# Gathering the neighbour features of 24 row tiles while the last block is still computed, and redoing up to ten listed rows of each partition

## The chip, the cores and the metric

The kernel runs on one core of a Trainium2 chip. The metric is the device time of one execution in microseconds (us). The kernel before was timed three times: 1668.05 us median, 1666.44 to 1670.25. One more execution was recorded by the hardware profiler; it took 1673.38 us, of which the recorded span is 1671.6 us.

## The reference, cut to what matters

Two layers over 4096 rows of 512 numbers. Layer 0 is an attention whose scores get the matrix `adj` added twice. Layer 1 is a graph attention in which every pair without an edge of weight 1 is pushed down by -1e10 times its distance from 1, so that for each row one neighbour wins alone: the column at which the row of `adj` is largest.

```python
def reference(x, adj, ...):
    # layer 0
    a = q @ k.T * scale + adj + adj
    x = layernorm(x + softmax(a) @ v)
    # layer 1, per head h
    feats = x @ W[h]
    dense = leaky_relu(e_self[:, None] + e_neigh[None, :]) + (-1e10) * (1 - adj)
    x = layernorm(x + relu(concat_h(softmax(dense) @ feats) + b))
```

## The kernel before, in words

The 4096 rows are 32 tiles of 128 rows (tile t holds rows 128t to 128t+127, one per partition) and eight blocks of four tiles. Layer 0 runs block by block; each block takes 32 chunks, each the 128 keys of one tile against the 512 queries of the block. A loop over steps s (two chunks each) issues scores, the subtraction of a maximum, exponentials, a split of each number into a high and a low half-precision part, and the products with the values. `NCP` is 128, the number of steps in which scores are made; the value products lag by `LAG` = 18 steps. The last 12 chunks (`TAIL`) are multiplied after the loop, one 128-query quarter at a time: first all 12 chunks for O0, then for O1, O2, O3.

When a block is finished, its four tiles go through eviction and statistics on VectorE (DVE), a four-instruction scaling on GpSimd (POOL, `scale_of`), the normalisation on ScalarE (ACT, `unit_rows`), the split, eight transposes on TensorE (PE), the product with the layer 1 weights (`feats`), and an eviction with the bias (`evict_feats`). The result, the features of the tile, is stored to `feats_scratch`; the layer 0 rows are stored to `x1_scratch` (the profile writes `x_scratch`). The four tiles of the last block are called J0 to J3 (tiles 28 to 31).

Beside this, DVE scans `adj` row by row and leaves in `pick[:, t]` the column of the largest entry of each row of tile t. After layer 0 the end phase gathers, by an indirect DMA per tile issued from POOL, the feature rows that `pick` names (line 741), adds them to the layer 0 rows (DVE, line 1601), computes squares (ACT, line 1167), the square root (line 1170), five short corrections (DVE, lines 1575 to 1587), and normalises the even tiles on ACT (line 1160) and the odd ones on DVE (line 1591). SyncE stores the result (line 584), four tiles at a time, the last four in two groups of two. POOL waits, before its first gather, until all 32 tiles of features are in memory (`f_out`).

DVE also computes a number that shows whether every row has one neighbour that wins alone (`prove_single`, lines 1427 to 1438). If the sum of it is not 4096, a general path over all pairs runs instead; it does not run on these inputs.

The order on each engine is the order in which the code is written; an engine waits in place for the semaphores of its next instruction, and what stands behind it waits too. Line 719 is POOL's running sum of the exponentials, line 731 POOL's DMA that adds the bias of v onto the rows of x, line 526 SyncE's load of those rows, line 1404 DVE's split of the last 20 chunks, line 1388 the eviction of O, line 1411 that of the features, line 888 the transposes, line 1107 `unit_rows`.

## Time and profile before

| What | Value |
|---|---|
| Median of three runs | 1668.05 us (1666.44 to 1670.25) |
| Profiled execution, its own time | 1673.38 us |
| Its span | 1671.6 us |
| PE, DVE, POOL, ACT busy | 93%, 73%, 52%, 32% of the span |
| Last matmul | about 1602 us |
| First gather of the end phase | 1605.11 us |

The span is the stretch between the first and the last recorded instruction. The busy shares are averages over stages with different limits: up to 1602 us PE is nearly always busy, and from there to the end it does nothing.

### The profile page before, as it was taken

The page shows a single profiled execution, that of the slowest core. Times are in us where ns is not written, and L with a number is a line of the kernel's source. Part 1 is how long each engine was busy: PE and PEld are TensorE (multiplying, and loading weights), DVE is VectorE, ACT ScalarE, POOL GpSimd, SP SyncE. Part 2 cuts the span into 40 slices and gives each one's busy share as a digit, 9 for nine tenths or more (in the row PEclk, how much of TensorE's full clock was granted, in tenths as well). Part 3 has the DMA queues.
Part 4 walks back from the last instruction along what each step waited for, and adds up shares of the span by engine and source line. Part 5 has one row for each costly group of instructions (what it writes and reads, how often), then busy time and mean ns, then how long its engine had stood idle before and what let it go on. Part 6 is the DMA issues. An engine that isn't in the chain of part 4 may idle for free.

```text
span 1671.6 us, 27914 instructions
## 1 busy us (share of the span) xinstructions
PE 1558.7 (93%) x10052; PEld 968.3 (58%) x10052; DVE 1219.5 (73%) x2438; ACT 539.9 (32%) x822; POOL 865.6 (52%) x809
## 2 busy tenths in 40 slices
PE   7999998999999999999999999999999999989830
PEld 3444686666666666666666666666666666644310
DVE  5898687688867876687768876788578867846445
ACT  4556301222232223222322223223322232236336
POOL 2987402556454645554545554564455545667343
PEclk9999999999999999999999999999999999999965
DMA  7467886779757886798669866897589757757357
GB/s 264 167 249 279 294 297 208 226 246 287 256 183 252 294 280 187 232 304 257 217 206 312 280 215 203 283 304 235 180 269 326 233 184 253 241 189 233 88 152 283
DMA packets 192396, 403.24 MB, mean 241 GB/s; under 512 B 20736, under 2 KB 26880, under 8 KB 191104
## 3 DMA queue, kind: packets, MB, share of 16 engines
q1 hardware_dynamic: 182912, 376.25, 67.3%
q0 software_dynamic: 9344, 25.17, 5.9%
q8 instruction: 81, 1.33, 0.3%
q14 instruction: 59, 0.48, 0.1%
HBM read 343.67 MB, written 57.67 MB: 240 GB/s over the span
## 4 chain that ended last, share of the span: by engine, by line
PE 81%; DVE 5%; DMA 5%; POOL 3%; issue 2%; ACT 2%; SPq 1%; another core or an unknown queue 0%; DVEq 0%; POOLq 0%; ACTq 0%
PE O L845 33%; PE S L804 30%; PE O L759 6%; PE X L759 5%; DMA yb<-y_scratch 3%; PE S L759 2%; PE O L804 2%; PE BC L759 1%; POOL work L719 1%; POOL ring L741 1%; PE X L888 1%; DVE work L1362 1%; DVE xr L1388 1%; DVE ring L1404 1%; POOL ring L709 1%
## 5 line engine op out<-in xcount | busy, mean ns | idle before, releaser
L845 PE MATMUL O<-vring,ring 128*128 128x512 f16 x2928 | 707.3, 379 | 4.7 <-POOL ring L709 3.6
L804 PE MATMUL S<-yb,big 128*128 128x256 f16 x4974 | 621.2, 273 | 15.9 <-DVE ring L1336 7.2
L709 POOL TENSOR_TENSOR ring<-work,ring 128x512 f16<-128x512 f32 x236 | 282.3, 1196 | 601.9 <-ACT ring L1020 601.9
L804 PEld LDWEIGHTS S<-yb,big 128*128 128x128 f16 x4974 | 482.9, 98 | 168.6 <-DVE ring L1336 10.9
L845 PEld LDWEIGHTS O<-vring,ring 128*128 128x128 f16 x2928 | 286.3, 98 | 261.5 <-issue 7.6
L1141 ACT ACTIVATE work<-ring 128x512 f32<-128x512 f32 x256 | 160.8, 628 | 750.7 <-DVE ring L1327 717.4
L1336 DVE TENSOR_TENSOR ring<-S,ring 128x256 f32<-128x256 f32 x476 | 199.6, 419 | 219.3 <-PE S L804 216.2
L719 POOL TENSOR_TENSOR work<-work 128x512 f32<-128x512 f32 x248 | 342.9, 1383 | 7.0 <-ACT work L1141 5.9
L1362 DVE TENSOR_TENSOR work<-work,ring 128x512 f32<-128x512 f32 x248 | 209.1, 843 | 0.6
L1341 DVE TENSOR_TENSOR ring<-S,ring 128x256 f32<-128x256 f32 x357 | 150.6, 422 | 63.9 <-PE S L804 47.6
L1327 DVE TENSOR_TENSOR ring<-BC,ring 128x512 f32<-128x512 f32 x256 | 173.6, 679 | 1.8 <-PE BC L873 1.8
L1300 DVE MAX8 cand<-big 128x8 f32<-128x512 f32 x256 | 171.2, 683 | 3.3 <-DMA big<-in_adj 2.0
L1020 ACT ACTIVATE ring<-work 128x512 f16<-128x512 f32 x259 | 164.8, 637 | 10.8 <-POOL work L672 2.6
L1020 ACT ACTIVATE work<-X 128x1024 f16<-128x1024 f16 x28 | 28.7, 1024 | 180.1 <-PE X L888 180.1
L759 PE MATMUL O<-big,ring 128*128 128x512 f16 x384 | 84.2, 379 | 0.0
L759 PE MATMUL X<-yb,work 128*128 128x512 f16 x336 | 77.1, 379 | 0.0
L759 PEld LDWEIGHTS O<-big,ring 128*128 128x128 f16 x384 | 37.6, 98 | 45.3
L759 PEld LDWEIGHTS X<-yb,work 128*128 128x128 f16 x336 | 32.5, 98 | 34.9 <-ACT work L1020 1.2
L689 POOL DMA_INDIRECT work<-in_adj,wonrow x32 | 32.8, 1024 | 32.2 <-DVE wonrow L1310 31.6
L759 PE MATMUL S<-ring,big 128*128 128x512 f16 x192 | 42.8, 379 | 1.8 <-DVE big L1197 1.8
L804 PE MATMUL O<-yb,big 128*128 128x256 f16 x354 | 44.2, 273 | 0.0
L741 POOL DMA_INDIRECT ring<-feats_scratch,pick x32 | 32.2, 1005 | 20.6 <-DMA feats_scratch<-xr 11.2
(145 smaller groups left out, 1094.4 us busy)
## 6 DMA issues: line engine op xcount, KB each, us to landing
ring<-in_adjT SPq DMA_DIRECT2D x256, 256.0 KB, 4.6
big<-in_adj SPq DMA_DIRECT2D x256, 256.0 KB
big<-x_scratch SPq DMA_DIRECT2D x126, 512.0 KB, 4.4
vring<-v_scratch SPq DMA_DIRECT2D x244, 256.0 KB
yb<-y_scratch SPq DMA_DIRECT2D x56, 256.0 KB, 6.3
y_scratch<-yb SPq DMA_DIRECT2D x7, 1792.0 KB, 10.6
ring<-in_xT SPq DMA_DIRECT2D x8, 1024.0 KB, 6.7
v_scratch<-vring SPq DMA_DIRECT2D x32, 256.0 KB, 2.6
```

Of the source, the lines that this page charges most:

```text
L709: pool.tensor_tensor(ring16[:, e % SLOTS, 1, :], pf[:, e % NPF, :], ring16[:, e % SLOTS, 0, :], ALU.subtract).then_inc(lo_done, 1)
L719: pool.tensor_tensor(sacc, sacc, pf[:, e % NPF, :], ALU.add).then_inc(sum_done, 1)
L759: mm = pe.matmul(psum, sta(a, k), mov(b, k), start=(k + a + b == 0), stop=(k == n - 1 and a == 1))
L804: mm = pe.matmul(bank, keys_of(p, keys, a, c), yb[:, b % 2, queries, m, c, :], start=(start and c + a + m == 0), stop=(c == 1 and a == 1), ...
L845: mm = pe.matmul(O[j][:, :], ring16[:, e % SLOTS, a, j * P:(j + 1) * P], values_of(e)[:, m, :], start=(k + a + m == 0), stop=(k == NT - 1 ...
L1020: return nc.scalar.activation(dst, src, ACT.Copy, scale=scale)
L1141: nc.scalar.activation(pf[:, e % NPF, :], ring[:, e % SLOTS, :], ACT.Exp, scale=-2.0).then_inc(exp_done, 1)
L1300: dve.max(cand[:, q, :], piece[:, p % NSC, :]).then_inc(cand_set, 1)
L1327: dve.tensor_tensor(slot, BC[:, :], slot, ALU.subtract).then_inc(sub_done, 1)
L1336: dve.tensor_tensor(dst, banks(p)[0], dst, ALU.add).then_inc(chain_read, 1)
L1341: dve.tensor_tensor(dst, banks(p)[1], dst, ALU.add).then_inc(side_read, 1)
L1362: dve.tensor_tensor(mx, mx, slot, ALU.max).then_inc(max_done, 1)
```

## The change

Features of tiles 0 to 23 (`TE` = 24) are now gathered before the last block's features exist. A row whose neighbour lies in the last block (row 3584 or above) can't be served by that, so DVE lists, for each partition, up to ten (`LK`) such rows among the 24 tiles (`late_rows`). The early gather reads some other row in their place, and the early result for them is stored like the others. The listed rows are then done a second time: their layer 0 rows are gathered again (`gather_x1`), their features are gathered when all are there, they go through the same arithmetic as columns of a tile, and an indirect DMA scatters them into the output over the early result (line 822). Empty places of the list read a fixed row and have a target row out of bounds, which the scatter leaves out. If a partition has more than ten such rows, the proof's number is lowered, and the general path runs.

The end phase has now 42 columns: 24 early tiles (groups 0 to 5), 10 listed columns (groups 6 to 8, of 4, 4 and 2), and the 8 tiles 24 to 31 (groups 9 and 10). The result is written over the layer 0 rows rather than over the gathered ones. Square roots and corrections are done for units of groups: (0,1,2), (3,4,5), (6,7,8), (9), (10). Seven semaphores less and some more: the bias load of q now shares the semaphore of the load of Wv, the load of W1 that of the small loads.

On the inputs of the reference (seed 0), 363 of the 3072 early rows have their neighbour in the last block, at most 6 in one partition; 917 of the 1280 places of the list stay empty.

The DVE order in the loop, where the last block is under way: statistics of a tile, then the eviction of features of another. Before:

```order
L1197 SCALAR_TENSOR_TENSOR work<-xr,work 128x512
L1327 TENSOR_TENSOR ring<-BC,ring 128x512
L1394 BN_STATS stats<-xr 128x6
L1396 BN_AGGR mv<-stats 128x2
L1411 SCALAR_TENSOR_TENSOR xr<-X,b1b 128x512
L1327 TENSOR_TENSOR ring<-BC,ring 128x512
```

The same place now (lines are those of the changed kernel; 1499 to 1516 are the old 1394 to 1411). Ten of the 18 added instructions are shown:

```order
L1499 BN_STATS stats<-xr 128x6
L1501 BN_AGGR mv<-stats 128x2
L1561 CAST yb<-pick 128x24
L1562 TENSOR_SCALAR yb<-yb 128x24
L1563 TENSOR_SCALAR early_pick<-yb 128x24
L1564 CAST yb<-tile_i 128x24
L1565 TENSOR_TENSOR yb<-yb 128x24
L1566 TENSOR_TENSOR yb<-yb 128x24
L1567 MAX yb<-yb 128x8
L1568 MATCH_REPLACE yb<-yb 128x24
L1569 MAX yb<-yb 128x8
L1571 TENSOR_SCALAR late_tile<-yb 128x10
```

The list stands between the statistics and the eviction of features, and each of its instructions waits for the one before.

POOL after the loop's last sums, before: four times the scaling of a tile, then 32 gathers in a row.

```order
L719 TENSOR_TENSOR work<-work 128x512 x6
L696 TENSOR_TENSOR ve<-mv,eps 128x1
L698 TENSOR_TENSOR rstd<-ve,mhalf 128x1
L699 TENSOR_TENSOR nmean<-mv,mone 128x1
L701 TENSOR_TENSOR nmean<-nmean,rstd 128x1
```

POOL now, from the last scaling (that of J3) on:

```order
L734 TENSOR_TENSOR ve<-mv,eps 128x1 [waits mv_set]
L736 TENSOR_TENSOR rstd<-ve,mhalf 128x1 [waits scale_set]
L737 TENSOR_TENSOR nmean<-mv,mone 128x1
L739 TENSOR_TENSOR nmean<-nmean,rstd 128x1 [waits scale_set]
L791 DMA ring<-feats_scratch,early_pick 128x512 [waits e_sum]
L791 DMA ring<-feats_scratch,early_pick 128x512 x3
L746 DMA work<-x_scratch,late_src 128x512 x3
L746 DMA vring<-x_scratch,late_src 128x512 x3
L814 DMA ring<-feats_scratch,late_pick 128x512 [waits pv_done,f_out]
L814 DMA ring<-feats_scratch,late_pick 128x512 x9
L814 DMA ring<-feats_scratch,pick 128x512 x8
L822 DMA out<-yb,late_row 3072x512 [waits e_out_odd,e_out,early_out]
```

Sixteen early gathers now stand between the sums and the last scaling, eight more behind it, then six gathers of layer 0 rows; only then come the 18 gathers that need the last features, and behind them ten scatters.

DVE between the evictions of J0 and J1, now (line 1709 is an addition, 1302 the split, 1493 an eviction of O):

```order
L1302 SCALAR_TENSOR_TENSOR work<-big,work 128x512
L1709 SCALAR_TENSOR_TENSOR big,yb<-ring,big 128x512 x4
L1712 TENSOR_SCALAR yb<-yb 128x4
L1493 SCALAR_TENSOR_TENSOR xr<-O,rinv,xr 128x512
L1499 BN_STATS stats<-xr 128x6
L1501 BN_AGGR mv<-stats 128x2
```

Before, the eviction stood right behind the split; four additions and a short instruction are now between them, and the same between J1 and J2 and between J2 and J3.

The diff, cut to its core:

```diff
+    TE = 24
+    LK = 10
@@ groups
+        GROUPS = [range(e * 4, e * 4 + 4) for e in range(TE // 4)] + [range(TE, TE + 4), range(TE + 4, TE + 8),
+                                                                     range(TE + 8, TE + LK)]
+        GROUPS += [range(TE + LK, TE + LK + 4), range(TE + LK + 4, TE + LK + 8)]
+        UNITS = ((0, 1, 2), (3, 4, 5), (6, 7, 8), (9,), (10,))
@@ SyncE
+            for e, columns in enumerate(GROUPS):
+                if e < GE or e >= GS:
+                    first, n = row_tile(columns[0]), len(columns)
+                    sp.wait_ge(e_out, (columns[-1] + 1) // 2)
+                    sp.wait_ge(e_out_odd, (columns[-1] + 1) // 2)
+                    sp.dma_start(out[first * P:(first + n) * P, :].rearrange("(j p) n -> p j n", p=P),
+                                 x1r[:, first:first + n, :]).then_inc(early_out if e < GE else out_done, 16)
@@ POOL, in the loop
+                if NCP + 9 <= s < NCP + 13:
+                    gather_x1(s - NCP - 9)
@@ POOL, behind the loop
-            for j in range(JB):
-                scale_of(NT - JB + j)
+            def gather_early(e):
+                if e == 0:
+                    pool.wait_ge(f_out, (NT - JB) * 16)
...
+                if e >= 3:
+                    pool.wait_ge(e_sum, GROUPS[e - 3][-1] + 1)
+                for c in GROUPS[e]:
+                    pool.indirect_dma_start(out=gathered(c), out_offset=None, in_=f_d[0:N - QB, :],
+                                            in_offset=bass.IndirectOffsetOnAxis(ap=early_pick[:, c:c + 1], axis=0)
+                                            ).then_inc(got_in[e], 16)
+            gather_early(0)
+            scale_of(J0)
+            gather_early(1)
+            scale_of(J1)
+            gather_early(2)
+            scale_of(J2)
+            gather_early(3)
+            scale_of(J3)
+            gather_early(4)
+            gather_early(5)
+            for k in range(4, LK):
+                gather_x1(k)
             pool.wait_ge(f_out, NT * 16)
...
+            pool.wait_ge(early_out, 16 * GE)
+            for e in range(GE, GS):
+                pool.wait_ge(e_out, (GROUPS[e][-1] + 1) // 2)
+                pool.wait_ge(e_out_odd, (GROUPS[e][-1] + 1) // 2)
+                for c in GROUPS[e]:
+                    pool.indirect_dma_start(out=out[0:TE * P, :],
+                                            out_offset=bass.IndirectOffsetOnAxis(ap=late_row[:, c - TE:c - TE + 1], axis=0),
+                                            in_=home(c), in_offset=None, bounds_check=TE * P - 1, oob_is_err=False
+                                            ).then_inc(late_moved, 16)
@@ ACT
             copy_transposed(first)
+            act.wait_ge(rinv_set, NB)
+            squares(0)
             unit_rows(first + 1, x1r[:, first + 1, :])
+            squares(1)
             copy_transposed(first + 1)
             unit_rows(first + 2, x1r[:, first + 2, :])
+            squares(2)
             unit_rows(first + 3, x1r[:, first + 3, :])
             copy_transposed(first + 2)
             copy_transposed(first + 3)
+            deviations(0)
+            squares(3)
+            squares(4)
+            squares(5)
+            deviations(1)
+            normalise(0)
+            squares(6)
+            normalise(1)
+            squares(7)
+            squares(8)
+            deviations(2)
+            squares(9)
+            deviations(3)
+            normalise(2)
+            squares(10)
+            deviations(4)
+            normalise(3)
+            normalise(4)
@@ DVE, in the loop
+                if s == NCP + 4:
+                    late_rows()
@@ DVE, behind the loop
             unit_rows_lo(J0, x1r[:, J0, :])
+            additions(0)
             evict(NB - 1, 1)
...
+            additions(1)
             evict(NB - 1, 2)
...
+            additions(2)
             evict(NB - 1, 3)
             statistics(J3)
             evict_feats(J0)
             unit_rows_lo(J3, x1r[:, J3, :])
             evict_feats(J1)
+            additions(3)
             evict_feats(J2)
             evict_feats(J3)
+            additions(4)
+            additions(5)
+            normalise_odd(0)
+            additions(6)
+            normalise_odd(1)
+            additions(7)
+            additions(8)
+            additions(9)
+            normalise_odd(2)
+            additions(10)
+            normalise_odd(3)
```

## Rows read from the trace of the kernel before

**Rows 1.** The page: its first line, and part 4, shares of the chain.

```profile
span 1671.6 us, 27914 instructions
PE 81%; DVE 5%; DMA 5%; POOL 3%; issue 2%; ACT 2%; SPq 1%; another core or an unknown queue 0%; DVEq 0%; POOLq 0%; ACTq 0%
```

**Rows 2.** Windows: length, busy PE, PEld, DVE, ACT, POOL (count), clock, DMA share, GB/s.

```profile
1610.00:1615.00 5.00, 0.00 (x0) 0.00 (x0) 2.06 (x7) 0.00 (x0) 3.78 (x5) 0.50 0.74 211
1640.00:1645.00 5.00, 0.00 (x0) 0.00 (x0) 0.96 (x6) 3.22 (x9) 3.78 (x5) 0.50 1.02 389
1655.00:1660.00 5.00, 0.00 (x0) 0.00 (x0) 4.72 (x17) 4.97 (x14) 0.00 (x0) 0.50 0.56 210
```

**Rows 3.** Timeline, 1596 to 1666: start, length, engine, line, what, idle before.

```profile
1596.28 0.62 PE L888 MATMUL S<-ident,work 128*128 128x128 f16 x8
...
1602.12 0.69 DVE L1411 SCALAR_TENSOR_TENSOR xr<-O,b1b 128x512 f32<-128x512 f32 x1 [1.90 <-PE O L759]
...
1605.11 1.11 POOL L741 DMA_INDIRECT ring<-feats_scratch,pick  x1 [11.18 <-DMA feats_scratch<-xr]
...
1612.94 0.69 DVE L1601 SCALAR_TENSOR_TENSOR ring<-ring,big 128x512 f32<-128x512 f32 x1 [10.13 <-DMA ring<-feats_scratch,pick]
...
1613.56 0.69 DVE L1601 SCALAR_TENSOR_TENSOR ring<-ring,big 128x512 f32<-128x512 f32 x1
...
1664.98 0.81 ACT L1160 ACTIVATE ring<-ring,yb 128x512 f32<-128x512 f32 x1 [0.31 <-DVE yb L1587]
```

**Rows 4.** The gathers, line 741, and the output stores, line 584: ns min/median/max.

```profile
L741 POOL DMA_INDIRECT ring<-feats_scratch,pick x32: 945/949/1402, 1605.1 to 1645.6; - x32
DMA to landing us min/median/max: 3.5/3.7/3.8
L584 SPq DMA_DIRECT2D out<-ring x9: 372/372/389, 1625.3 to 1665.8; - x9
```

**Rows 5.** Timeline, 1499 to 1504, where the list is put.

```profile
1499.81 3.83 PE L845 MATMUL O<-vring,ring 128*128 128x512 f16 x17
1500.87 0.18 DVE L1396 BATCH_NORM_AGGREGATE mv<-stats 128x2 f32<-128x6 f32 x1
1500.97 0.69 DVE L1411 SCALAR_TENSOR_TENSOR xr<-X,b1b 128x512 f32<-128x512 f32 x1
1503.48 0.61 PE L888 MATMUL X<-ident,work 128*128 128x128 f16 x8
```

**Rows 6.** Timeline, dependent short DVE instructions: at 1251 and 1524.

```profile
1251.05 0.22 DVE L1304 MAX8 top<-cand 128x8 f32<-128x64 f32 x1
1251.37 0.09 DVE L1306 MATCH_VALUE_LOAD wonq<-top,cand 128x8 f32 x1
1524.43 1.07 DVE L1430 TENSOR_SCALAR yb<-top 128x64 f32<-128x64 f32 x1
1526.53 0.19 DVE L1436 TENSOR_TENSOR yb<-yb 128x32 f32<-128x32 f32 x1
1526.76 0.19 DVE L1437 TENSOR_TENSOR yb<-yb 128x32 f32<-128x32 f32 x1
```

**Rows 7.** Timeline, 1547 to 1560, before the last quarter products.

```profile
1547.52 1.47 POOL L719 TENSOR_TENSOR work<-work 128x512 f32<-128x512 f32 x1 [0.21 <-ACT work L1141]
1548.11 1.75 SPq L526 DMA_DIRECT2D xr<-in_x  x4
1554.23 1.38 POOL L731 DMA_DIRECT2D xr<-in_bv  x1 [5.24 <-DMA xr<-in_x]
```

**Rows 8.** Timeline, 1565 to 1591: J0, and the eviction of J3.

```profile
1565.22 1.05 PE L856 MATMUL X<-vup,work 128*128 128x1 f32 x8 [0.22 <-POOL work L719]
...
1568.37 0.19 POOL L696 TENSOR_TENSOR ve<-mv,eps 128x1 f32<-128x1 f32 x1 [3.21 <-DVE mv L1396]
...
1574.12 0.62 PE L888 MATMUL S<-ident,work 128*128 128x128 f16 x8
...
1590.84 0.75 DVE L1388 SCALAR_TENSOR_TENSOR xr<-O,rinv,xr 128x512 f32<-128x512 f32 x1 [2.83 <-PE O L845]
```

More of the change, by code:

```diff
@@ new lines, in adj_resnorm_kernel, with row_tile @@
+        e_s = end[:, 384:384 + 64]
+        e_r = end[:, 448:448 + 64]
+        e_t = end[:, 512:512 + 64]
+        e_nm = end[:, 576:576 + 64]
+        e_tot = end[:, 640:640 + 64]
+        okw = end[:, 1024:1024 + 8 * NT]
+        late = end[:, 1280:1536]
+        def row_tile(c):
+            return c if c < TE else c - LK
+        x1s = [end[:, 1536 + D * k:1536 + D * (k + 1)] for k in range(4)]
+        x1s += [mx, diag.rearrange("p j n -> p (j n)"), won]
+        x1s += [vring[:, k].rearrange("p a n -> p (a n)").bitcast(F32) for k in range(NV)]
@@ L579, in _ @@
             store_feats(J3)
[L580 to L586 removed]
+            for e, columns in enumerate(GROUPS):
[5 more added lines that the diff above has]
+                                 x1r[:, first:first + n, :]).then_inc(early_out if e < GE else out_done, 16)
+            sp.wait_ge(early_out, 16 * GE)
+            sp.wait_ge(out_done, 16 * (NE - GS))
+            sp.wait_ge(late_moved, 16 * 2 * LK)
             for j in range(JB):
```

236 lines of the change are left out of this document (141 added, 95 removed).

## The prediction

> **What bounds the kernel now.** I read the page first, then the windows of the end, then the timeline of the hand-over. The chain of waits is PE for 81% of the span [rows 1]: until the last matmul the kernel is bound by PE, and work added beside PE costs nothing unless PE waits for it. Behind it comes an end phase of another kind. The last feature eviction starts at 1602.12, the first gather at 1605.11, when the features are in memory, and the span ends at 1671.6: 66.5 us without a matmul [rows 1, 3]. In it POOL issues 32 gathers, the first at 1605.1, the last at 1645.6: 40.5 / 31 = 1.31 us from one to the next, though one is busy for 0.95 only [rows 4]. DVE makes its first addition at 1612.94, waiting for a gather [rows 3]. The DMA engines are not full at first (211 GB/s at 1610), are full at 1640 (share 1.02, 389 GB/s) and half full at 1655 [rows 2]. So the end is bound first by POOL's issue, then by DMA, then by ACT and DVE, with a last store at 1665.8 that ends 5.8 us later [rows 1, 4]. The change starts this phase 40 us earlier for three quarters of the tiles, and adds 20 indirect DMAs and 10 columns of arithmetic.
>
> All times below are on the clock of the profiled execution.
>
> **Part 1, the list on DVE: +3.7 us.** Eighteen dependent instructions are put between the statistics and the eviction of features, at 1501.05 [rows 5]. No row shows one of them in this place. Dependent short ones follow each other by 0.23 us (1526.53 to 1526.76), and by 0.32 where a pause instruction stands between, as it does in the list (1251.05 to 1251.37) [rows 6]. I take 0.30, nearer to the second: 5.4 us. Behind them the eviction of features waits, and for it the transposes of the next tile, on PE in order. The eviction ended at 1500.97 + 0.69 = 1501.66, while PE has matmuls until 1503.4 [rows 5]; the cover is 1.7 us. PE waits 5.4 - 1.7 = 3.7 us and has no slack to win it back before the load of x for the last block, which is released by PE's progress. Low end: 18 x 0.23 - 1.7 = 2.4. High end: 18 x 0.32 and one slow first instruction, as the 1.07 us one in the proof (0.9 over its likes) [rows 6]: 5.8 + 0.9 - 1.7 = 5.0. The two steps added to the proof (0.5 us) fall where DVE is not waited for by PE.
>
> **Part 2, four gathers of layer 0 rows inside the loop: 0.** They cost POOL 4 x 1.31 = 5.2 us between its last sums. POOL has 0.21 us idle before each sum there, and 5.24 us of idle time before line 731, where it waits for x [rows 7]. Eight sums' idle time takes 1.7, the other 3.5 lie in the 5.24. SyncE issues the load by PE's progress, so POOL's delay does not move it. That leaves 1.2 us of cover.
>
> **Part 3, early work beside the last block's tiles: 0, though the features come 3.5 us later.** POOL is free at 1565.2, and the first statistics reach it at 1568.37 [rows 8]. Four gathers end at 1570.5, so the scaling of J0 is 2.1 us late; its rows, split, are ready just when PE reaches their transposes at 1574.12. On DVE a group of additions is 4 x 0.62 (1612.94 to 1613.56) + 0.2 = 2.7 us [rows 3]. Walking DVE, ACT and POOL in their new order, the evictions of J1, J2 and J3 start at 1577.0, 1585.1 and 1594.0 (the last was 1590.84 [rows 8]). PE does not wait for J1 and J2; the transposes of J3 go from 1596.28 to 1599.4 [rows 3], and the last features reach memory at 1608.6 and not 1605.1. This is hidden by the next part, which is later.
>
> **Part 4, POOL's way to the gathers that matter: +10.3 us.** J3's scaling can end at 1597.1 (statistics 1595.8, scaling 1.3). Behind it stand eight early gathers and six of layer 0 rows: 14 x 1.31 = 18.3, so the 18 gathers that need the last features start at 1615.4, not at 1605.1. Here the queue has turned into the bound: 3.3 of the 10.3 would be the features' own lateness anyway.
>
> **Part 5, from there to the end: 47.1 us and not 66.5, -19.4 us.** 18 gathers take 23.6: until 1639.0. But POOL then waits for the early stores. The first three (ACT normalises after the squares of groups 3 to 5) can go at 1620.7, the next three at 1633.3. From 1620.7 DMA has 6 x 1.05 MB of stores and 14 gathers x 0.26 MB, 9.9 MB, at 389 GB/s [rows 2] 25.5 us; with a landing, 1646.7. The listed columns are normalised at about 1645.9, so the store is what releases. Ten scatters at the gather's 1.31 start until 1646.7 + 9 x 1.31 = 1658.5 and land 3.7 later [rows 4], 1662.2, the end at 1662.5. The last store (four tiles, ready at 1651.9) lands by 1659.2, taking the old 5.8 us plus 1.5 for twice the bytes: it isn't the last. The scatter is an operation that before does not show. From below it is 0.95 us, POOL's busy time for a gather; then that store ends the kernel, -3.3 us. From above twice a gather, 2.6 us: +11.6 us. I take the gather's.
>
> The Trainium skill (DMA: Bandwidth & Descriptors, Bandwidth) puts the HBM side at about 358 GB/s per core. The row of 389 GB/s is above it, so the trace does not agree here; by the page's figure part 5 would end 2.2 us later, by an estimate.
>
> The merged semaphores in the first 20 us I cost at nothing: the bias waits now for Wv, behind PE's first product.
>
> **Sum.** +3.7 + 10.3 - 19.4 = -5.4 us: 1673.38 - 5.4 = 1668.0 for an execution like the profiled one. That one is 5.3 us above the median of the timed runs, so I put the same difference on the median: 1668.05 - 5.4 = 1662.6 us.
>
> **Rivals.** (a) The scatter is dearer than a gather: it has a bound to check per row. From 1.31 + 5.4 / 9 = 1.9 us each the gain is gone; at 2.6 it is 1662.6 + 11.6 = 1674.2 us, slower. For it speaks that all ten stand alone at the very end, with nothing beside them. Against: seven in ten of their rows move nothing. Chance 0.18. (b) The stores don't get 389 GB/s. That rate stood in the fullest stretch only; 9.9 MB at 320 GB/s take 31 us and end 5.4 later: 1668, no change. Gathers in the same queues then land later too. Chance 0.17. (c) More is won: the list costs 2.4 and scatters 0.95 each: 1662.6 - 1.3 - 3.3 = 1658 us. For it speaks that empty rows of a scatter make no transfer. Chance 0.22. (d) The cover of part 2 fails, since the list delays DVE, ACT and POOL more than it does PE: POOL reaches the x load later than the load lands, up to 3.5 us, and each late us moves the whole end: 1666. Chance 0.05. (e) The change does not do what it says, and the general path runs: it needs more than ten listed rows in a partition, and the inputs have at most 6. Chance 0. The forecast keeps 0.38.
>
> **The numbers.** A measurement of this kernel can tell about 0.2%, 3.3 us. Faster by more: nearly all of the forecast (0.33), (c), and 0.03 of the others: 0.57. Within: 0.05 of the forecast, most of (b) and of (d): 0.22. Slower by more: (a), and the worst of (b) and (d): 0.21. The forecast's own range is 1659 to 1666; the range from (c) with something over to where (a) is at 2.5 us each is 1655 to 1673.
>
> **What would show it.** In the profile after: DVE's list of about 5.4 us before the eviction of features at 1501, and PE idle for 3.7 before the transposes behind it; POOL still idle before line 780 (old 731); the 18 late gathers starting at about 1619 (1615.4 + 3.7); early stores issued at about 1624 and 1637; the ten scatters last on POOL, 1.3 us apart, from about 1650; a span of 1666. I am wrong if the scatters are far from 1.3 us, if PE does not wait behind the list, or if ACT or DVE and not POOL's scatters end the kernel.

## The result and the profile after

The changed kernel takes 1687.41 us (median of four runs) against 1669.15 for the kernel before (four runs, 1666.44 to 1671.62). One of the four, at 2112.58 us and a lower clock, was disturbed and is left out of the ratio; the others lie between 1683.43 and 1687.67. The ratio is 1.0102, with a 95% interval of 1.0084 to 1.0119: the kernel is slower by 1%, 25 us above the forecast of 1662.6. The profiled execution took 1683.43 us and has a span of 1681.6, where the one before had 1673.38 and 1671.6 [rows 1].

Walk along the same marks as the forecast did. The first is the list. The timeline of the changed kernel (start, length, engine, line, operation):

```profile
1500.47 0.32 DVE L1561 CAST yb<-pick 128x24 f32<-128x24 uint32 x1
1500.72 1.27 POOL L766 TENSOR_TENSOR work<-work 128x512 f32<-128x512 f32 x1
1500.90 1.12 DVE L1562 TENSOR_SCALAR yb<-yb 128x24 f32<-128x24 f32 x1
1501.94 1.16 POOL L756 TENSOR_TENSOR ring<-work,ring 128x512 f16<-128x512 f32 x1
1502.13 1.01 DVE L1563 TENSOR_SCALAR early_pick<-yb 128x24 uint32<-128x24 f32 x1
1503.06 1.26 POOL L766 TENSOR_TENSOR work<-work 128x512 f32<-128x512 f32 x1
1503.24 1.12 DVE L1564 CAST yb<-tile_i 128x24 f32<-128x24 int32 x1
1504.46 0.18 DVE L1565 TENSOR_TENSOR yb<-yb 128x24 f32<-128x24 f32 x1
...
1506.24 0.17 DVE L1572 CAST yb<-late_tile 128x10 f32<-128x10 int32 x1
...
1508.52 0.69 DVE L1516 SCALAR_TENSOR_TENSOR xr<-X,b1b 128x512 f32<-128x512 f32 x1 [0.17 <-DVE late_src L1581]
1509.36 1.01 PE L970 MATMUL X<-ident,work 128*128 128x128 f16 x8 [5.85 <-DVE xr L1516]
```

Eighteen steps take 8.0 us (1500.47 to 1508.52), not 5.4. Fifteen of them follow each other by 0.28 us or a little more. Lines 1562, 1563 and 1564 take 1.0 to 1.1 us each, although they touch 24 elements, and each ends within 0.1 us of the end of POOL's long addition or subtraction beside it. PE waits 5.85 us for the eviction of features, where before it waited for nothing [rows 5], and behind that wait it runs at the lower of its two clocks, 1.2 GHz (granted clock 0.50 from 1509 to 1513, 1.00 from there): six matmuls in 2.77 us instead of 1.46. The second mark is the hand-over to the last quarter products, the answer to [rows 7] and to the first row of [rows 8]:

```profile
1542.64 1.15 DVE L1509 TENSOR_TENSOR ring<-work,ring 128x512 f16<-128x512 f32 x1
1543.41 1.32 POOL L746 DMA_INDIRECT yb<-x_scratch,late_src  x1 [0.17 <-POOL work L766]
1544.32 2.29 DVE L1509 TENSOR_TENSOR ring<-work,ring 128x512 f16<-128x512 f32 x1
...
1555.43 1.75 SPq L560 DMA_DIRECT2D xr<-in_x  x4
...
1562.87 1.42 POOL L780 DMA_DIRECT2D xr<-in_bv  x1 [2.03 <-DMA xr<-in_x]
1563.35 2.80 DVE L1509 TENSOR_TENSOR ring<-work,ring 128x512 f16<-128x512 f32 x1 [0.16 <-ACT ring L1102]
...
1574.08 1.05 PE L938 MATMUL X<-vup,work 128*128 128x1 f32 x8 [0.22 <-POOL work L766]
```

POOL still has 2.03 us of idle time before line 780, which adds bv, though no longer 5.24. DVE's line 1509 takes 2.29 us when a gather of POOL stands beside it, 1.15 beside POOL's sums, and 0.68 at 1561.92, where POOL does nothing. The row sums come at 1574.08 instead of 1565.22. The third mark is the end phase, the answer to [rows 2 to 4]:

```profile
1616.17 0.69 DVE L1516 SCALAR_TENSOR_TENSOR xr<-O,b1b 128x512 f32<-128x512 f32 x1 [1.90 <-PE O L841]
...
1624.56 0.94 POOL L814 DMA_INDIRECT ring<-feats_scratch,late_pick  x1 [0.30 <-issue]
...
1659.19 1.51 ACT L1245 ACTIVATE yb<-yb 128x512 f32<-128x512 f32 x2
...
1663.53 1.03 POOL L822 DMA_INDIRECT out<-yb,late_row  x1 [16.04 <-DVE big L1738]
...
1675.19 0.98 POOL L822 DMA_INDIRECT out<-vring,late_row  x1 [0.30 <-issue]
```

In windows (length, busy PE, PEld, DVE, ACT, POOL, clock, DMA share, GB/s):

```profile
1625.00:1630.00 5.00, 0.00 (x0) 0.00 (x0) 2.63 (x6) 4.90 (x11) 3.78 (x5) 0.50 0.90 201
1640.00:1645.00 5.00, 0.00 (x0) 0.00 (x0) 1.06 (x3) 4.83 (x8) 3.90 (x4) 0.50 1.04 222
1655.00:1660.00 5.00, 0.00 (x0) 0.00 (x0) 4.79 (x16) 4.28 (x11) 0.00 (x0) 0.50 1.00 391
```

The lines of the late gathers (L814) and of the scatters (L822); the MOVE is what POOL's queue runs ahead of each scatter:

```profile
L814 POOL DMA_INDIRECT ring<-feats_scratch,late_pick x10: 942/946/1316, 1624.6 to 1636.3; - x10
DMA to landing us min/median/max: 5.0/9.4/12.5
L822 POOLq MOVE  x10: 29/29/29, 1662.2 to 1667.8; - x10
L822 POOL DMA_INDIRECT out<-vring,late_row x3: 985/987/987, 1672.6 to 1675.2; - x3
DMA to landing us min/median/max: 2.1/3.6/6.7
```

Late gathers land 9.4 us after their issue (median), where before they took 3.7. The first scatter starts 39.0 us behind the first late gather; ten of them start 1.29 us apart, as forecast; the span ends 6.4 us after the last start.

The profile's name for what released the first scatter (DVE's line 1738) can't be right, for that instruction ends at 1663.46 and POOL's queue has been past its waits since 1662.2. By the kernel, POOL waits there for the six early stores and then for the listed columns of the first group only, two of which ACT normalises. ACT has done the second of them at 1660.70 (1659.19 + 1.51). The DMA engines move the last bytes of the stores between 1661.5 and 1662.0 (share 0.07, then 0.00). So the stores are what comes last here, by 1.5 us, as the forecast had it, and the first scatter starts 1.3 us behind the release.

One more thing is new: from 1625 to 1660 the DMA engines are busy all the time (share 0.90 to 1.04), but move 201 GB/s at 1625 and 222 at 1640, against 391 at 1655 with the same share.

**e8_after_again.** The changed kernel was run again beside the experiments.

> The changed kernel itself, beside the same runs of the kernel before: ratio 1.010 as on the other chip, if the loss does not hang on the chip. In its profile the waits at the list (PE 5.9 us), before the row sums, and at the first scatter (16 us) should come again.

Measured on another chip: 1689.34 us (4 runs), ratio 1.007 (1.0052 to 1.0089), so the loss is there again, somewhat smaller. The experiments ran on four chips, each beside runs of the kernel before, so ratios and not times are compared. So that profiles can be compared, I count from one mark ahead of the list, the start of the two matmuls S<-usum (1483.60 before, 1483.11 after). Each figure is the difference of two starts in the timeline, in us:

| kernel | mark to row sums | to last feature eviction | to first late gather | to first scatter | to last scatter | to the end |
|---|---|---|---|---|---|---|
| before | 81.6 | 36.9 | 3.0 (first gather) | | | 66.5 |
| after | 91.0 | 42.1 | 8.4 | 39.0 | 11.7 | 6.4 |
| after, second profile (e8) | 91.9 | 44.5 | 5.8 | 44.6 | 11.6 | 6.5 |
| e1 spread | 91.8 | 41.2 | 8.4 | 38.8 | 11.7 | 6.4 |
| e2 list split | 83.1 | 43.6 | 6.9 | 39.9 | 11.8 | 6.4 |
| e10 thin stores | 90.7 | 41.2 | 8.5 | 38.8 | 11.6 | 6.5 |
| e12 spread, thin stores | 92.2 | 43.6 | 6.9 | 40.2 | 11.6 | 6.5 |
| e15 list split, pause | 84.7 | 42.2 | 11.7 | 38.8 | 11.6 | 6.4 |
| e5 six places | 84.9 | 46.3 | 3.8 | 33.3 | 6.5 | 7.8 |
| e7 six, spread, order | 83.1 | 43.8 | 5.2 | 32.7 | 6.6 | 8.1 |
| e9 six, stores sooner | 82.8 | 43.6 | 5.0 | 29.9 | 7.0 | 9.0 |

### The profile page after: what moved, and what is told of

Read it like the earlier page. It is cut to its first block and busy times, and to the rows that moved or that the text cites. A ratio compares the mean times of both kernels' runs of the same rounds, so it can differ in the third digit from the quotient of the medians.

```text
span 1681.6 us, 28033 instructions
## 1 busy us (share of the span) xinstructions
PE 1563.7 (93%) x10052; PEld 970.2 (58%) x10052; DVE 1239.5 (74%) x2466; ACT 552.2 (33%) x843; POOL 895.8 (53%) x840
## 5 line engine op out<-in xcount | busy, mean ns | idle before, releaser
L841 PEld LDWEIGHTS O<-big,ring 128*128 128x128 f16 x384 | 37.6, 98 | 45.3
L927 PE MATMUL O<-ring 128*128 128x512 f16 x144 | 35.4, 399 | 7.0 <-DVE ring L1509 7.0
```

What stands on the lines that cost most here:

```text
L841: mm = pe.matmul(psum, sta(a, k), mov(b, k), start=(k + a + b == 0), stop=(k == n - 1 and a == 1))
L927: mm = pe.matmul(O[j][:, :], ring16[:, e % SLOTS, a, j * P:(j + 1) * P], values_of(e)[:, m, :], start=(k + a + m == 0), stop=(k == NT - 1 ...
```

## Experiments on the list and inside the loop

**e2_list_split.** The changed kernel with the list in two halves of nine steps, behind DVE's first subtraction of the next two steps instead of ahead of an eviction:

```diff
-                if s == NCP + 4:
-                    late_rows()
+                subtract(e)
+                if s in (NCP + 5, NCP + 6):
+                    late_rows(s - NCP - 5)
```

> The changed kernel, but the 18 instructions of the list stand in two halves of nine behind the first subtraction of steps NCP+5 and NCP+6, where DVE was idle for 5.4 us in the kernel before. Theory (the list costs what PE waits behind it): PE's wait of 5.9 us before the transposes at 1509 is gone, and with it the 1.3 us of half clock behind it; the last sums end 6.5 to 7.5 us earlier, and so does the kernel. Rival (the list is hidden anyway by the load of x, POOL's sums or the early gathers, and moving it only moves the wait): less than 2 us.

Measured: 1679.12 us (10 runs), ratio 1.0019 (1.0006 to 1.0032). From the mark to the run of 108 matmuls behind the list it is 40.9 us (1487.40 to 1528.33), as before (1483.60 to 1524.57, 41.0), against 48.8 in the changed kernel (1483.11 to 1531.89). So the list in one piece cost 7.8 us of the path, and in two pieces nothing. Its trace also settles why three steps are slow. The CAST of tile_i took 1.12 us at 1503.24 above; here it is line 1566:

```profile
1508.57 0.18 POOL L735 TENSOR_TENSOR ve<-mv,eps 128x1 f32<-128x1 f32 x1
1508.74 0.18 DVE L1566 CAST yb<-tile_i 128x24 f32<-128x24 int32 x1
...
1514.99 1.15 POOL L757 TENSOR_TENSOR ring<-work,ring 128x512 f16<-128x512 f32 x1
1515.16 1.01 DVE L1574 CAST yb<-late_tile 128x10 f32<-128x10 int32 x1
```

The same CAST takes 0.18 us beside a short instruction of POOL. The CAST of late_tile, 0.17 us at 1506.24 above, takes 1.01 now that it has fallen beside POOL's line 757. Not the operation, but POOL's 128x512 work at the same time makes a step 1.1 us long. The Trainium skill (SBUF — State Buffer, "Who interferes with whom") states that copies, casts and tensor_scalar of DVE in their two-port modes take a pair of ports that it shares with GpSimd, as an exclusive lock for a whole instruction, so that whoever comes second waits until the first is done; the rows agree, each of the three ending with POOL's instruction. Row sums still come 1.5 us later than before (83.1 against 81.6), which is the price of what else the change puts there: the four gathers inside the loop and two more steps in the proof.

**e3_x1_sooner.** The changed kernel with those gathers four steps sooner:

```diff
-                if NCP + 9 <= s < NCP + 13:
-                    gather_x1(s - NCP - 9)
+                if NCP + 5 <= s < NCP + 9:
+                    gather_x1(s - NCP - 5)
```

> The changed kernel, but the four gathers of layer 0 rows in the loop stand at steps NCP+5 to NCP+8, where POOL waits for ACT, and not at NCP+9 to NCP+12 between its last sums. Theory (each of the four holds DVE's split of a chunk, 2.2 us instead of 1.16, and the delay outlasts the load of x): the row sums come 1 to 2 us earlier, the kernel 1 to 2 us. Rival (their cover holds, as I costed it): no change within 0.5 us.

Measured: 1686.43 us (4 runs), ratio 1.0063 (1.0042 to 1.0083), not to be told from the changed kernel's 1.007 of e8. From the run of 108 matmuls to the row sums it is 42.7 us (1534.38 to 1577.08), no less than 42.2 after, and 40.7 before. Their place among POOL's last sums is not what costs the 1.5 us.

## Experiments on the end phase

**e4_before_one_row.** The kernel before, with eight of its 32 gathers (tiles 4 to 11) reading one and the same row in all partitions:

```diff
+                    rows = one_row[:, 0:1] if 4 <= t < 12 else pick[:, t:t + 1]
-                                            in_offset=bass.IndirectOffsetOnAxis(ap=pick[:, t:t + 1], axis=0)
+                                            in_offset=bass.IndirectOffsetOnAxis(ap=rows, axis=0)
```

> The kernel before, but the eight gathers of tiles 4 to 11 read row 4095 in all 128 partitions in place of their picks, so these tiles of the result are not the reference's. It measures the price of reading one row by itself: the gathers stand early in the end phase, when DMA is not full (211 GB/s before). Theory (one row is slow): they land in 6 us or more, DMA share is near 1 at 200 GB/s or less, and the end comes 5 us or more later. Rival: they land in 3.7 us as the others, no change.

Measured: one execution, 1678.43 us with a span of 1676.6. Its time shows nothing, for the kernel before had a median of 1676.85 (1670.95 to 1679.15) beside it. The first gather starts at 1603.24, so it is 73.4 us from there to the end, against 66.5 in the first profile of the kernel before and 70.2 in its second (e14 below). Nor is all of that the price of one row: in this profile DVE stands still from 1631.9 to 1646.7 but for a few short instructions, a thing that comes up again below and that the profiles of the kernel before have too, for 8.5 and 12 us. What comes ahead of it is the gathers' own: the third and the fourth group of additions start 21.5 and 26.2 us behind the first gather, against 18.2 and 23.9 in both profiles of the kernel before, 2.3 to 3.3 us later. The windows of this kernel:

```profile
1615.00:1620.00 5.00, 0.00 (x0) 0.00 (x0) 2.52 (x8) 3.33 (x8) 3.78 (x5) 0.50 0.94 155
1620.00:1625.00 5.00, 0.00 (x0) 0.00 (x0) 2.19 (x11) 4.64 (x11) 3.83 (x4) 0.50 0.89 202
```

The engines are 0.94 and 0.89 busy for 155 and 202 GB/s, where before had 0.69 and 0.72 for 201 and 197. A gather of one row by 128 partitions holds the engines longer for the same bytes.

**e1_spread.** The changed kernel, with empty places of the list pointing at rows that differ from partition to partition (three steps more):

```diff
+                then(dve.tensor_scalar(filler, top[:, 0:LK], 0.0, -1.0, ALU.is_equal, ALU.mult))
+                then(dve.scalar_tensor_tensor(out=none, in0=filler, scalar=rowf[:, :], in1=none, op0=ALU.mult, op1=ALU.add))
```

> The changed kernel, but what fills an empty place is another row for each partition: an empty place of the list reads feature row 4095 - 8p (about) and layer 0 row p instead of 4095 and 3071 for all, and an early row with a late neighbour reads the row 512 above it instead of 3583. Three more short instructions in the list (+0.8 us). Theory (many reads of one row are slow, whatever the engines' busy share says): from 1635 to 1645 DMA moves over 370 GB/s and not 222 to 301, the late gathers land within 6 us instead of up to 12.5, the wait before the first scatter falls from 16 us to 9 or less, and the time falls by 5 to 8 us against the changed kernel. Rival (the low rate comes from stores and gathers in one queue, or from the number of gathers): the rates stay, the time rises by 0.8 us.

Measured: 1688.68 us (4 runs), ratio 1.0081 (1.006 to 1.0101): no gain. Early rows with a late neighbour and the empty places of the layer 0 gathers are spread in the same way (not shown in the cut). The slow transfers are gone:

```profile
1635.00:1640.00 5.00, 0.00 (x0) 0.00 (x0) 3.17 (x7) 4.91 (x10) 3.78 (x5) 0.50 1.04 395
1640.00:1645.00 5.00, 0.00 (x0) 0.00 (x0) 2.12 (x7) 1.76 (x3) 3.78 (x5) 0.50 1.03 404
```

395 and 404 GB/s, against 301 and 222 after, and no transfers from 1655 on (share 0.05). So the stores no longer come last: POOL's queue is past its waits at 1660.4, right behind the end of ACT's second listed normalisation at 1660.29. Yet the first scatter stays 38.8 us behind the first late gather, for ACT itself waits 8.10 us at 1649.87 for DVE, which between 1642 and 1649.7 starts an instruction each 1.40 us and then none for 2.80 us.

**e10_thin_stores.** The changed kernel, with the six early stores writing 8 of 128 rows of each tile:

```diff
+                    m = 8 if e < GE else P
-                                 x1r[:, first:first + n, :])
+                                 x1r[0:m, first:first + n, :])
```

> The changed kernel, with the six early stores writing 8 of 128 rows of each tile, so 0.4 MB instead of 6.3 MB; the other rows of those tiles are left out. Theory 1 (the full DMA engines are why the late gathers land late, the stalls of DVE and ACT come and the first scatter waits): late gathers land in under 4 us as in the kernel before, no stall stands on DVE from 1634 to 1655, the first scatter starts as soon as ACT has normalised the list, some 31 us behind the first late gather as forecast, not 39 to 45, and the span is 8 to 10 us shorter than with whole stores. Theory 2 (the gathers of one row hold the engines by themselves): DMA share stays near 1 with under 250 GB/s from 1625 to 1645, and at most 3 us are won.

Measured: one execution, span 1681.7, first scatter 38.8 us behind the first late gather (the 37.5 in the expectation of e12 counts from the second gather, a slip of mine), so no gain from 5.9 MB less. Without the stores ACT's normalisation is what comes last: it ends at 1662.21, POOL's queue goes on at 1662.3. But ACT comes 37.4 us behind the first late gather here, against 36.1 in the changed kernel, and DVE starts one instruction each 1.40 us or none from 1636 to 1639.6 and again from 1644 to 1651.6, as in e1 and unlike in the first profile of the changed kernel. What thin stores bring without that, this run does not show.

**e11_no_scatters.** The changed kernel without its ten scatters. 

> The changed kernel with the ten scatters left out, so the listed rows keep what the early stores wrote. It gives what the scatters cost at the end, where they stand alone. Forecast's view: ten scatters of 1.29 us and their landing are all that stands behind the last store, which is issued at about 1669: the span becomes that issue and 6 us, 5 to 7 us less than with them. Other view: SP's last waits and the end of the program take the 6.4 us between the last scatter's start and the end, scatter or store alike, and less than 5 us are won.

Measured: span 1677.9, 196.1 us from the mark, against 198.5 and 204.8 in the two profiles of the changed kernel. The last store is issued at 1670.9 and the span ends 7.0 later. With scatters it was issued at 1669.6 and the span ended 12.0 later: they cost 5 us at the end, as the first of the two views had it. This profile has the standstill of e1 too (1634.1 to 1645.2), so the spans themselves can't be compared to a microsecond.

**e12_spread_thin.** Both edits together. 

> The changed kernel with ten places, with both suspects of the end phase gone: empty places read spread rows, and the early stores write 8 of 128 rows of each tile (the rest of those tiles is left out). Neither alone brought more than 2 us. Theory 1 (either of the two is enough to fill the DMA engines, so only both together free the end): no window from 1625 to 1650 shows a DMA share over 0.8, late gathers land in under 4 us, DVE has no stall, and the first scatter starts 31 us behind the first late gather, as forecast (39.0 in the changed kernel, 38.8 with spread reads, 37.5 with thin stores): some 7 us less than the changed kernel, ratio near 1.003. Theory 2 (DVE and ACT stand still in this stretch for a reason that isn't the transfers): stalls of 5 us or more stay in DVE's rows with the engines half empty, and the first scatter stays over 36 us behind.

Measured: 1687.11 us, ratio 1.0073 (1.005 to 1.0096), first scatter 40.2 us behind. The windows and the timeline of DVE:

```profile
1635.00:1640.00 5.00, 0.00 (x0) 0.00 (x0) 1.10 (x5) 0.00 (x0) 3.78 (x5) 0.50 0.71 233
1640.00:1645.00 5.00, 0.00 (x0) 0.00 (x0) 0.57 (x4) 3.25 (x8) 3.78 (x5) 0.50 0.73 206
```

```profile
1635.34 0.69 DVE L1716 SCALAR_TENSOR_TENSOR yb<-ring,yb 128x512 f32<-128x512 f32 x1
...
1639.93 0.17 DVE L1719 TENSOR_SCALAR yb<-yb 128x4 f32<-128x4 f32 x1 [3.90 <-remote]
...
1642.74 0.17 DVE L1727 SCALAR_TENSOR_TENSOR yb<-yb 128x12 f32<-128x12 f32 x1 [2.51 <-issue]
1644.13 0.17 DVE L1730 SCALAR_TENSOR_TENSOR yb<-yb 128x12 f32<-128x12 f32 x1 [1.22 <-DVE yb L1727]
1645.53 0.17 DVE L1733 SCALAR_TENSOR_TENSOR yb<-yb 128x12 f32<-128x12 f32 x1 [1.23 <-DVE yb L1730]
1646.93 0.17 DVE L1737 SCALAR_TENSOR_TENSOR yb<-yb 128x12 f32<-128x12 f32 x1 [1.23 <-DVE yb L1733]
1648.34 2.83 DVE L1745 TENSOR_SCALAR big<-big,yb 128x512 f32<-128x512 f32 x6 [1.24 <-issue]
```

The engines are used to 0.71 and 0.73 only, and DVE stands still all the same: for 3.90 us with nothing to wait for that the profile shows, and then one instruction each 1.40 us, chained 128x12 instructions that follow each other by 0.2 us elsewhere. ACT resumes at the same instant, 1648.34. POOL starts its last gather at 1647.21; after it all is quick again. The kernel before shows the like, unremarked by me at the forecast: from 1637.6 to 1646.1 its DVE runs six short instructions and nothing else, and this lies in its 66.5 us.

**e14_before_again** and **e13_before_pause.** The kernel before once more, and the kernel before with a break of 4 us on POOL behind its 16th gather:

```diff
+                if e == 4:
+                    pause()    # 3 x pool.tensor_tensor(sacc, sacc, sacc, ALU.subtract), each waited for
```

> The kernel before itself, for a second profile of it. Theory 1: DVE's standstill comes again at the same place, after 25 or so gathers. Theory 2 (chance of the execution): it is gone, longer, or elsewhere.

> The kernel before, with three dependent additions of 128x512 on POOL, some 4 us, between its 16th and 17th gather. In its profile DVE and ACT stand still from 1637.7 to 1646.1 with their semaphores reached, starting one instruction per 1.40 us, and the stretch begins some 25 gathers after POOL began to issue them without a break. Theory 1 (a long unbroken row of indirect DMAs brings the standstill, whether the engines are full or not): the break takes it away, DVE shows no idle time put to nothing, and the end comes no later than before, although 16 gathers start 4 us later: ratio 0.998 to 1.000. Theory 2 (it comes by chance of the execution, or by DVE's place in its program): it stays, and the 4 us are lost: ratio 1.0025.

Measured: e14 has the standstill at the same place, from 1639.0 to 1651, 26 gathers into the row; span 1676.6. In e13 it is gone, and from the first gather to the end it is 64.3 us, against 66.5 and 70.2 with the standstill. 1673.65 us (12 runs) with a ratio of 0.9991 (0.9975 to 1.0006) say the same without a profile: the 4 us of delay came back. The window of 1640 to 1645, first of e14, then of e13:

```profile
1640.00:1645.00 5.00, 0.00 (x0) 0.00 (x0) 0.00 (x0) 0.00 (x0) 3.78 (x4) 0.50 1.03 402
```

```profile
1640.00:1645.00 5.00, 0.00 (x0) 0.00 (x0) 4.44 (x16) 1.87 (x5) 3.88 (x4) 0.50 1.01 367
```

DVE and ACT run nothing for 5 us in the one, and 16 and 5 instructions in the other, both with full DMA engines (1.03 and 1.01).

**e15_split_pause.** The same break in the kernel of e2, ahead of its 18 late gathers. 

> The changed kernel with the list in two halves (ratio 1.0019 by itself), and the same 4 us break on POOL between its 14 gathers behind J3's scaling and the 18 late ones. By itself POOL issued 32 without a break, and DVE stood still from 1631.6 to 1642. Theory 1: the standstill goes, the first scatter starts 31 us behind the first late gather instead of 39.9, and with the 4 us lost the kernel is 4 to 5 us faster than without the break: ratio 0.999. Theory 2: it stays, and 4 us are lost: ratio 1.004.

Measured: 1680.69 us (12 runs), ratio 1.0033 (1.0019 to 1.0046). The standstill is gone, but the time isn't: DVE waits 9.4 and 1.8 us for late gathers, and the engines move 198 and 151 GB/s at a share of 1.00 and 0.99 from 1635 to 1645. Here the stores come last again: ACT's second listed normalisation ends at 1657.08, the DMA engines are done by 1659 (share 0.58, 0.07 and 0.00 in the microseconds from 1657), and POOL's queue goes on at 1659.0. The first scatter is 38.8 us behind, as in e1. The kernel that would settle it, with spread reads and the break, was not built.

## Fewer places: a version that is faster than both

**e5_six**, **e6_six_spread**, **e7_six_order**, **e9_store_sooner.** All have the list in two halves, and six places instead of ten (the inputs need six; a seventh sends a partition's rows to the general path):

```diff
-    LK = 10
+    LK = 6
-        UNITS = ((0, 1, 2), (3, 4, 5), (6, 7, 8), (9,), (10,))
+        UNITS = ((0, 1, 2), (3, 4, 5), (6, 7), (8,), (9,))
```

e6 adds the spread reads of e1; e7 lets ACT and DVE normalise the listed columns ahead of the next four tiles; e9 also normalises the first twelve tiles sooner:

```diff
             squares(3)
+            normalise(0)
             squares(4)
             squares(5)
             deviations(1)
-            normalise(0)
```

> The list has room for six rows of a partition instead of ten (the inputs need six at most), and is made in two halves as in the experiment before; 16 steps, for the second maximum and its replacement aren't needed. Four gathers of layer 0 rows, four gathers of features, four scatters and four columns of arithmetic are gone. Theory 1 (the end is bound by how many indirect DMAs POOL issues one after another): the late gathers start 4 x 1.26 = 5.0 us sooner and the scatters are 4 x 1.29 = 5.2 us shorter, together 10.2 us: 1669 us of span against 1679.1 with ten, ratio to before 0.996. Theory 2 (the first scatter is set by transfers and by ACT, the four layer 0 gathers are hidden): only the scatters' 5.2 us are won: span 1674, ratio 0.999. Theory 3 (the last store and not the scatters then ends the kernel): a gain between the two, and the last DMA to land is that store.

> The same with six places, and empty places of the list read rows spread over the tensor instead of one row. Theory 1 (reads of one row by 128 partitions are what holds the DMA engines at 200 GB/s): of six columns at least three are nearly empty, so those 2 x 3 gathers land sooner, the windows from the early stores on show 380 GB/s or more, and the end comes 2 to 4 us sooner than with six places alone: ratio 0.994. Theory 2 (ACT's and DVE's order sets the first scatter): DMA rates rise but the end stays within 1 us of the kernel with six places alone.

> The kernel before it, with ACT and DVE normalising the listed columns before they take the first four tiles of the last block, not behind them. Theory 2: the first scatter waits for ACT, so it starts about 3.4 us sooner (four squares of 0.85), and the end 2 to 3 us sooner, until the last store ends it. Theory 1: the first scatter waits for the early stores to land, and nothing changes; the last store comes later by the time that was moved, 1 to 2 us, which costs as much if it is the end.

> The kernel with six places, spread reads and the listed columns normalised first; ACT now normalises the first twelve tiles before the squares of group 4 and DVE its half behind the last feature eviction. In the kernel before it ACT idles 5.5 us at 1608.5 and the DMA engines are used to 0.32 from 1615 to 1620, while the first early store is issued at 1622.6 and all stand full from 1625 to 1645. Theory 1 (the first scatter waits for the early stores, 1648.6): the first three stores are issued about 8 us sooner, DMA is done about 6 us sooner, the first scatter starts at about 1642 and the last store, bound by ACT, ends the kernel: 3 to 5 us less, ratio to before 0.990 to 0.991. Theory 2 (stores and late gathers then collide sooner, and the gathers, on which DVE waits, land later by what the stores win): no change, ratio 0.993.

| kernel | median us, runs | ratio to before, interval |
|---|---|---|
| e5_six | 1667.27, 5 | 0.9938, 0.9923 to 0.9953 |
| e6_six_spread | 1666.17, 5 | 0.9932, 0.9917 to 0.9948 |
| e7_six_order | 1665.37, 5 | 0.9933, 0.9916 to 0.9950 |
| e9_store_sooner | 1665.37, 5 | 0.9932, 0.9918 to 0.9946 |

The kernel before had a median of 1677 us beside them. From the first late gather to the end e5 takes 47.6 us and e7 47.3, where after took 57.0. Six places bring 0.8% over ten (0.9938 against 1.0019), some 13.6 us, more than the 10.2 us of issue that were counted: in all four profiles POOL has 3.7 to 4.2 us of idle time ahead of its late gathers, since it waits for the last features, and DVE and ACT do not stand still behind it. (The two ratios come from two chips.) In all four the early stores release the first scatter, 3.0 to 8.9 us behind ACT's normalisation, which is why e7's new order of ACT brings nothing. Spread reads, the order of ACT and earlier stores each move a row of the profile as expected and the time by less than can be measured. In e9 the first store goes at 1613.9 instead of 1622.6 and the window of 1615 to 1620 fills:

```profile
1615.00:1620.00 5.00, 0.00 (x0) 0.00 (x0) 4.79 (x17) 4.75 (x13) 3.37 (x3) 0.50 0.32 79
```

```profile
1615.00:1620.00 5.00, 0.00 (x0) 0.00 (x0) 4.96 (x16) 1.62 (x4) 2.19 (x2) 0.50 1.00 370
```

From 79 (e7) to 370 GB/s (e9); but DVE then waits 7.5 us for the first late gathers instead of 3.4, behind those stores in the same engines, and the rival of that expectation is right.

## Why the forecast was wrong

**Bounds.** Right: up to the last matmul PE is the bound, and each microsecond put on it (list, clock, gathers) reached the end.

**Part 1, the list: +3.7 forecast, +7.8 measured** (48.8 against 41.0 from the mark). Mechanism right, size wrong twice. The range for the list ended at 5.8 us and allowed for one slow first instruction; 15 steps went at 0.28 and three at 1.1, beside POOL. The row of 1.07 us in [rows 6] was the hint: I read it as a first instruction that is slow, when a neighbour on POOL is what makes one slow. And after 5.85 us of waiting PE runs some 2 us behind at half its clock, which the sum left out.

**Part 2, gathers in the loop: 0 forecast, 1.5 measured.** The cover held: POOL still waits 2.03 us for x before line 780. (The forecast's own numbers leave 5.24 - 3.5 = 1.7 us of it, not 1.2.) So rival (d), by which POOL would come later than the load, did not happen in this profile. What the sum left out is the load itself. It is issued 23.5 us behind the start of the 108 matmuls in both kernels (1548.11 and 1555.43), but POOL goes on 7.44 us behind its issue instead of 6.12. That is 1.3 of the 1.5 us, and e2 has the same 7.45. It is not so everywhere: in e1 and e10 POOL goes on 6.25 and 5.66 us behind the issue, and the row sums come 18.7 and 18.2 us behind it all the same, against 17.1 before. So the 1.5 us are there in all of them, and which wait they lie in is not settled.

**Part 3, beside the last block: features 3.5 us later forecast, 5.2 measured** (42.1 against 36.9), 1.2 of it because 24 matmuls of the last features ran partly at the lower clock (6.53 us instead of 5.34, granted clock 0.80 from 1610 to 1615). It stood behind part 4 and was hidden, as said.

**Part 4, POOL's way: right.** From the row sums to the first late gather the forecast had 50.2 us (1615.4 less 1565.22), the profile has 50.5.

**Part 5 is the step that failed: 47.1 us from the first late gather to the end forecast, 57.0 measured.** Scatters at 1.31 each: right (1.29), so rival (a) did not happen. Their tail: 6.4 us behind the last start, not 4.0; the forecast let the landing of a gather stand for that of a scatter and for the end of the program. The rest, 7.7 us, lies ahead of the first scatter, and the term that failed is the transfers of the early stores. The forecast had them issued 5.3 and 17.9 us behind the first late gather, and the profile has 4.2 and 17.5. It gave 9.9 MB 25.5 us at 389 GB/s. The profile has 10.95 MB between 1628.8 and 1662.0, at a mean of 330 GB/s: 33.2 us, for the windows of 1635 and 1640 bring only 301 and 222. So the release comes 37.6 us behind the first late gather and not 31.3, and the scatter starts 1.3 us behind its release, which no term had. This is rival (b), with its place, its size (320 GB/s) and its sign that gathers land later (9.4 us); it had a chance of 0.17, and it did not know why the rate falls.

The 358 GB/s that the forecast takes from the Trainium skill (DMA: Bandwidth & Descriptors, Bandwidth) is there a core's share while both cores of its pair stream. This kernel runs on one core, so the row of 389 does not speak against the page.

The second term ahead of the first scatter failed as well, and was hidden by 1.5 us only. It had the listed columns normalised 30.5 us behind the first late gather; ACT has done those of the first group 36.1 us behind it, in e10 37.4, in e1 37.3. So there are two ways to the first scatter, the stores and the chain of late gather, addition, square and normalisation, and both are some 6 us too long. Two things stretch them: reads of one row by the empty places (after, e15), which slow the stores and the late gathers, and the standstill of DVE and ACT in a long row of gathers (e1, e10, e12), which slows the chain. The second profile of the changed kernel has both, and 44.6 us. Taking one away let the other set the end, which is how I read that e1, e10, e12 and e15 brought nothing. Each of the two is shown by itself: the standstill goes with a break on POOL (e13, e15), the low rate goes with spread rows (windows of e1). That the two together are the whole of the loss is argued and not shown, for no kernel with ten places has neither, and 31 us were never seen with ten.

**The account.** The profiled span was to become 1666.2 (1671.6 - 5.4) and became 1681.6, 15.4 us more: row sums 8.9 later instead of 3.7 (+5.2), part 4 +0.3, first scatter +7.7, scatters -0.1, tail +2.4, together 15.5. The timed median is off by 24.8 us (1687.41 - 1662.6), and the other 9.4 lie outside this profile. The forecast took 5.3 us off, since the profiled execution of the kernel before was slower than the median; that of the changed kernel is 4.0 us faster than its median (1683.43). It is also the only one of its two profiles without the standstill, so the others may well have had it; their times alone can't show that.

**What stays open.** What the standstill is. It came in both profiles of the kernel before, after 26 gathers without a break, and in that of e4 after 23; in seven of the eight profiles of kernels with ten places and no break, some 24 gathers into the row behind J3's scaling (e1, e2, e3, e8, e10, e11, e12); it did not come in the first profile of the changed kernel, whose row is as long, nor in any where POOL paused for some 4 us. A shorter one, of 2.9 to 5.1 us, stands ahead of one of the last two feature evictions in the profiles of e3, e5, e6, e7, e8, e10 and e11, also some 22 gathers behind POOL's first early one, though there with breaks of 2 to 3 us in between; it makes the second column of the table vary. A queue that fills would look so, but no row shows one. It is seen in recorded executions only; that it is no effect of the recording rests on the times of e13. Open too are what the 1.5 us of part 2 are made of, and what ten places cost with spread reads and a break.

## What to carry to other kernels

Short dependent instructions on DVE cost what POOL is doing beside them: price them at the row of the neighbour (1.1 us here), not at their own 0.2, and put them where DVE's successors are not waited for. An indirect DMA for places that are empty is not free: it costs its issue, its arithmetic and, when all partitions point at one row, engine time; the first thing to cut was the number of places, worth 0.8%. When two waits end within 1.5 us of each other, taking one away shows nothing of its price. And before a stage is timed by its parts, look at whether its rows hold idle time that nothing explains: a stage that has 8 us of it will not shrink as the sum says.

## What the runs showed of the chip that was not expected

- Gathers in which all partitions read one row of 2 KB: eight of them made the additions behind them start 2.3 to 3.3 us later (e4), with DMA share 0.94 at 155 GB/s; spread rows brought 395 and 404 GB/s (e1) where one row had 301 and 222.
- DVE and ACT standing still for some microseconds, then or in between one instruction each 1.40 us, 5 to 15 us in all, behind some 23 to 26 indirect DMAs that POOL issued without a break; gone with 4 us of other work on POOL between them (e13, e15), with the DMA engines as full as before.
- DVE's 128x512 TENSOR_TENSOR with both inputs in SBUF takes 2.2 to 2.3 us when an indirect DMA of POOL is issued beside it, 1.16 beside POOL's own 128x512 sum, 0.68 beside nothing.
- Landing of an indirect DMA: 3.5 to 3.8 us alone, 5.0 to 12.5 beside stores.
